# Three reorderings in a two-layer perceiver block: the opening, the last fp4 tile, and a copy in the second attention

## The reference

```
x = x + L0_xattn(ln(x), ctx, ctx, mask)   # 16 heads of 32, 512 keys a batch, projections Wq, Wk, Wv, Wo
x = x + L0_attn(ln(x))                    # RWKV-6 time mix
x = x + L0_ffn(ln(x))                     # gate, up (512 -> 1408), down; fp4 quantise-dequantise of all operands
x = x + L1_xattn(ln(x), ctx, ctx)         # 16 heads of 32, no projections
x = x + L1_attn(ln(x))                    # banded projections, sparse mask
x = x + L1_ffn(ln(x))                     # ternary weights, 512 -> 2048 -> 512
```

## Time and profile before

| | us |
|---|---|
| median of 3 runs | 1557.14 (1554.85 to 1558.16) |
| the profiled execution, its own time | 1559.67 |
| its span, first to last instruction | 1557.9 |
| opening, 0 to 50 | 50 |
| first attention, 50 to 465 | 415 |
| fp4 layer to the start of the second attention, up to | 1142 |
| second attention, from 1142 to | 1317.6 |

### The profile page before, as it was taken

One profiled execution on the slowest core, in us unless ns is written; L12 is line 12 of the kernel. 1 busy time (PEld: TensorE's weight loads), 2 busy tenths in 40 slices (PEclk: granted clock), 3 DMA queues, 4 the chain that ended last, 5 costly groups with the idle time before them and its releaser, 6 DMA issues. The chain is left out here.

```text
span 1557.9 us, 33173 instructions
## 1 busy us (share of the span) xinstructions
PE 1422.0 (91%) x13826; PEld 930.6 (60%) x13826; DVE 1113.0 (71%) x2268; ACT 620.1 (40%) x1285; POOL 183.1 (12%) x179
## 2 busy tenths in 40 slices
PE   6999999999999997999769999999889898978898
PEld 3677777777777776434465644444445555667453
DVE  6477777777787887760497887677558787575787
ACT  2455444554445442223103411110168786034643
POOL 2300000000000000130001000000000001153800
PEclk9999999999999999999989999999899999989999
DMA  6353444444455433400005200000045461040000
GB/s 254 110 178 135 146 148 142 144 146 142 163 171 182 137 107 117 142 1 0 2 27 201 108 1 1 0 0 0 0 163 208 174 229 43 1 165 2 1 28 28
DMA packets 55449, 153.65 MB, mean 99 GB/s; under 512 B 11997, under 2 KB 16861, under 8 KB 49162
## 3 DMA queue, kind: packets, MB, share of 16 engines
q1 hardware_dynamic: 50186, 134.82, 25.0%
q0 software_dynamic: 5120, 16.78, 2.7%
HBM read 117.73 MB, written 33.85 MB: 97 GB/s over the span
## 5 line engine op out<-in xcount | busy, mean ns | idle before, releaser
L744 ACT ACTIVATE l0x_prob<-l0x_prob,l0x_negmax 128x512 f32<-128x512 f32 x128 | 90.9, 712 | 114.8 <-DVE l0x_negmax L818 114.8
L602 PE MATMUL bank<-l0x_upper_v,l0x_ctxT 128*128 128x512 f32 x256 | 106.6, 416 | 2.1 <-DVE l0x_V L797 2.1
L589 PE MATMUL bank<-l0x_ctxT,l0x_upper_k 128*128 128x512 f32 x256 | 106.7, 417 | 1.3 <-PEq L284 1.3
L604 PE MATMUL bank<-l0x_upper_v,l0x_ctxT_lower 128*128 128x512 f32 x256 | 101.6, 397 | 0.0
L603 PE MATMUL bank<-l0x_lower_v,l0x_ctxT 128*128 128x512 f32 x256 | 101.3, 396 | 0.0
L591 PE MATMUL bank<-l0x_ctxT,l0x_lower_k 128*128 128x512 f32 x256 | 100.7, 393 | 0.0
L590 PE MATMUL bank<-l0x_ctxT_lower,l0x_upper_k 128*128 128x512 f32 x256 | 100.2, 391 | 0.0
L1166 DVE CUSTOM_DVE_ANT_0 l1x_prob<-bank,l1x_zeros 128x512 f32<-128x512 f32 x128 | 80.8, 687 | 26.6 <-PE bank L1034 26.0
L1047 PE MATMUL bank<-ident,l1x_prob 128*128 128x128 f32 x512 | 81.5, 289 | 11.9 <-ACT l1x_prob L1117 8.4
L1117 ACT ACTIVATE l1x_prob<-l1x_prob,l1x_negmax 128x512 f32<-128x512 f32 x128 | 91.1, 714 | 1.0 <-DVE l1x_negmax L1166 1.0
L1930 ACT ACTIVATE f_silu<-bank 128x512 f32<-128x512 f32 (+1 forms) x24 | 13.5, 562 | 190.4 <-PE bank L1873 184.1
(11 more groups left out here) (335 smaller groups left out, 3094.1 us busy)
## 6 DMA issues: line engine op xcount, KB each, us to landing
l0x_ctx<-in_ctx SPq DMA_DIRECT2D x16, 1024.0 KB, 5.2
turned_context<-l0x_whole POOLq DMA_DIRECT2D x64, 256.0 KB, 2.4
l1x_KT<-turned_context SPq DMA_DIRECT2D x16, 1024.0 KB, 7.0
l1x_ctx<-in_ctx SPq DMA_DIRECT2D x16, 1024.0 KB, 4.8
fp_weight<-l0x_weight_piece SPq DMA_DIRECT2D x24, 352.0 KB, 4.8
f_raw<-fp_weight SPq DMA_DIRECT2D x3, 2816.0 KB, 18.5
l0x_abs_piece<-in_L_ffn_w_gate SPq DMA_DIRECT2D x16, 512.0 KB, 4.0
l0x_abs_piece<-in_L_ffn_w_up SPq DMA_DIRECT2D x16, 512.0 KB, 5.4
```

Source lines behind the costliest of these rows:

```text
L589: nc.tensor.matmul(bank[:, :], w.upper_k[:, kc, cols], c, start=kc == 0, stop=False)
L602: nc.tensor.matmul(bank[:, :], c, w.upper_v[:, kc, :], start=kc == 0, stop=False)
L604: last = nc.tensor.matmul(bank[:, :], c_lower, w.upper_v[:, kc, :], start=False, stop=kc == CH - 1)
L744: nc.scalar.activation(w.prob[r][:, :], w.prob[r][:, :], ACT.Exp, scale=-1.0, bias=w.negmax[:, p:p + 1], accum_out=w.rowsum[:, b % 2, p:p ...
```

## The change

- The three opening blocks become one, `opening`. Statistics and normalising are done in two halves of four tiles. PE first makes 20 products of a tile of ones, then turns tiles 0 to 3, makes query products 0 and 1, turns tiles 4 to 7, gathers the columns, and goes on with products 2 to 7; the first context turn follows product 2. All eight copies to `g.XNT` are ACT's. The memset of the ones moves here from `projected_attention`.
- The last fp4 tile turns, copies and multiplies its three pieces one after the other (`last_tile`), through the gate banks and into `work[0]`. The rows of tiles 0 to 6 are turned after it. The addition of its sum to `g.X` and the statistics move to the front of DVE's list in `cross_attention`, ahead of the last tile's aggregate.
- In the second attention `heads_copy` stands behind the second exponential on ACT, and `turn_back` behind the second turn on PE.

```diff
@@ -294,30 +287,73 @@
 
         @block.tensor
         def _(pe):
-            def turn(c):
+            def turn_rows(t):
+
+                pe.wait_ge(normed, t + 1)
+                if t >= HALF_TILES:
+                    pe.wait_ge(rows_copied, 2 if t < 6 else t - 1)
+                for c in range(CH):
+                    last = nc.tensor.transpose(g.bank[TURN_BANKS[t]][:, c * P:(c + 1) * P], g.XN[:, t, c * P:(c + 1) * P],
+                                               g.ident[:, :])
+                last.then_inc(rows_turned, 1)
+
+            def turn_context(c):
 
                 pe.wait_ge(w.ctx_loaded[0], 16)
                 if c >= 2:
                     pe.wait_ge(w.whole_ready, c - 1)
+                else:
+                    pe.wait_ge(rows_copied, TILES)
                 for kc in range(KC):
                     last = nc.tensor.transpose(turn_bank[c % 2][:, kc * P:(kc + 1) * P], w.ctx[0][:, kc, c * P:(c + 1) * P],
                                                g.ident[:, :])
                 last.then_inc(turned, 1)
 
-            pe.wait_ge(w.query_weights_loaded, 16)
-            for j in range(8):
+            def query(j):
+
                 oc, half = j % CH, j // CH
+                pe.wait_ge(rows_copied, HALF_TILES * (half + 1))
                 if j >= 6:
                     pe.wait_ge(done, j - 5)
                 for kc in range(CH):
                     last = nc.tensor.matmul(query_bank[j % 6][:, :], w.Wq[:, kc, oc * P:(oc + 1) * P],
                                             g.XNT[:, kc, half * 512:(half + 1) * 512], start=kc == 0, stop=kc == CH - 1)
                 last.then_inc(summed, 1)
+
+
+            pe.wait_ge(w.ones_done, 1)
+            for _ in range(20):
+                nc.tensor.matmul(g.bank[0][:, 0:P], w.ones[:, :], w.ones[:, :], start=True, stop=True)
+            pe.wait_ge(g.ident_loaded, 16)
+            for t in range(HALF_TILES):
+                turn_rows(t)
+            pe.wait_ge(w.query_weights_loaded, 16)
+            query(0)
+            query(1)
+            for t in range(HALF_TILES, TILES):
+                turn_rows(t)
+            pe.wait_ge(g.loaded, 16 * NAMES)
+            for c in range(CH):
+                nc.tensor.transpose(g.bank[3][:, c * 16:c * 16 + NAMES], g.vec[0:NAMES, c * P:(c + 1) * P],
+                                    g.ident[0:NAMES, 0:NAMES]).then_inc(gathered, 1)
+            query(2)
+            turn_context(0)
+            pe.wait_ge(columns_copied, 2)
+            for j in range(3, 8):
...
@@ -331,6 +367,24 @@
 
         @block.vector
         def _(dve):
+            def normalise(half):
+
+                lo, hi = half * HALF_TILES, (half + 1) * HALF_TILES
+                for t in range(lo, hi):
+                    dve.wait_ge(g.x_loaded[t // (TILES // X_PARTS)], 16)
+                    nc.vector.bn_stats(g.stats[:, t, :], g.X[:, t, :]).then_inc(stats_done, 1)
+                dve.wait_ge(stats_done, hi)
+                for t in range(lo, hi):
+                    nc.vector.bn_aggr(g.mean_var[:, t, :], g.stats[:, t, :]).then_inc(aggr_done, 1)
+                dve.wait_ge(aggr_done, hi)
+                nc.vector.tensor_scalar(g.rstd[:, 0, lo:hi], g.mean_var[:, lo:hi, 1], LN_EPS, None, ALU.add).then_inc(var_eps, 1)
+                dve.wait_ge(std_done, half + 1)
+                nc.vector.reciprocal(g.rstd[:, 2, lo:hi], g.rstd[:, 1, lo:hi]).then_inc(rstd_done, 1)
+                dve.wait_ge(rstd_done, half + 1)
+                for t in range(lo, hi):
+                    nc.vector.tensor_scalar(g.XN[:, t, :], g.X[:, t, :], g.mean_var[:, t, 0:1], g.rstd[:, 2, t:t + 1],
+                                            ALU.subtract, ALU.mult).then_inc(normed, 1)
+
             def weight_upper(i, weight):
 
                 dve.wait_ge(w.weight_loaded[i], 16)
@@ -349,6 +403,13 @@
                 dve.wait_ge(w.ctx_upper, c + 1)
                 nc.vector.tensor_tensor(w.ctxT_lower[0][:, c, :], whole[:, :], w.upper[:, :], ALU.subtract).then_inc(w.ctx_lower, 1)
 
+            normalise(0)
+            normalise(1)
+            nc.vector.tensor_copy(g.ident16[:, :], g.ident[:, :]).then_inc(columns_copied, 1)
+            dve.wait_ge(gathered, CH)
+            nc.vector.tensor_copy(g.columns[:, :, 0:NAMES],
+                                  g.bank[3][:, 0:CH * 16].rearrange("p (c n) -> p c n", c=CH)[:, :, 0:NAMES]).then_inc(columns_copied, 1)
+            dve.wait_ge(columns_copied, 2)
             dve.wait_ge(w.mask_rows_loaded, 16)
             nc.vector.tensor_scalar(w.mask_scaled.rearrange("b (c k) -> b c k", c=KC),
...
@@ -1088,9 +1150,9 @@
             scores(0)
             for k in range(QUADS):
                 turn_probabilities(k, 0)
+                turn_probabilities(k, 1)
                 if k % 2 == 1 and k > 1:
                     turn_back(k // 2 - 1)
-                turn_probabilities(k, 1)
                 if k + 1 < QUADS:
                     scores(k + 1)
                 turn_probabilities(k, 2)
@@ -1133,9 +1195,9 @@
             nc.scalar.activation(g.rstd[:, 1, final:TILES], g.rstd[:, 0, final:TILES], ACT.Sqrt).then_inc(last_std, 1)
             for k in range(QUADS):
                 exponential(k, 0)
+                exponential(k, 1)
                 if k % 2 == 1 and k > 1:
                     heads_copy(k // 2 - 1)
-                exponential(k, 1)
                 turned_copy(k, 0)
                 exponential(k, 2)
                 if copied_by_scalar(k, 1):
@@ -1215,6 +1277,10 @@
                     nc.vector.tensor_scalar(g.XN[:, t, :], g.X[:, t, :], g.mean_var[:, t, 0:1], g.rstd[:, 2, t:t + 1],
                                             ALU.subtract, ALU.mult).then_inc(normed, 1)
 
+            nc.vector.tensor_tensor(g.X[:, final, :], g.X[:, final, :], g.bank[6][:, :], ALU.add).then_inc(last_summed, 1)
+            dve.wait_ge(last_summed, 1)
+            nc.vector.bn_stats(g.stats[:, final, :], g.X[:, final, :]).then_inc(last_stats, 1)
+            dve.wait_ge(last_stats, 1)
             nc.vector.bn_aggr(g.mean_var[:, final, :], g.stats[:, final, :]).then_inc(last_aggr, 1)
             dve.wait_ge(last_aggr, 1)
...
@@ -1804,6 +1868,7 @@
         s(f"head_{n}") for n in ("aggr", "eps", "std", "rstd", "normed", "turned", "copied"))
     R = len(N0)
     gate, up, work = g.bank[0:3], g.bank[3:6], g.bank[6:8]
+    LAST_OUT, HEAD_BANKS = work[0], up + gate + [work[1]]
 
     def over_tiles(eng, body):
@@ -1874,23 +1939,41 @@
                                                     start=kc == 0, stop=kc == CH - 1)
                     last.then_inc(gate_up_full, 1)
 
+            def last_tile(t):
+
+                for r, (at, n) in enumerate(N0):
+                    pe.wait_ge(step, t * (R * Q_STEPS) + (r + 1) * Q_STEPS)
+                    for c in range(n // P):
+                        ins = nc.tensor.transpose(gate[r][:, c * P:(c + 1) * P], w.hq[:, at + c * P:at + (c + 1) * P],
+                                                  g.ident[:, :])
+                    ins.then_inc(turn_full, 1)
+                    pe.wait_ge(turned, t * R + r + 1)
+                    for kc in range(at // P, (at + n) // P):
+                        ins = nc.tensor.matmul(LAST_OUT[:, :], w.hT[:, kc * P:(kc + 1) * P], w.downT[:, kc, :],
+                                               start=kc == 0, stop=kc == IC0 - 1)
+                ins.then_inc(out_full, 1)
+                pe.wait_ge(x_done, t)
+                turn_rows()
+
             def turn_rows():
 
                 for t in range(HEAD_TILES):
                     pe.wait_ge(head_normed, t + 1)
                     for c in range(CH):
-                        ins = nc.tensor.transpose(g.bank[t][:, c * P:(c + 1) * P], g.XN[:, t, c * P:(c + 1) * P], g.ident[:, :])
+                        ins = nc.tensor.transpose(HEAD_BANKS[t][:, c * P:(c + 1) * P], g.XN[:, t, c * P:(c + 1) * P], g.ident[:, :])
                     ins.then_inc(rows_turned, 1)
 
             def body(t, first, last, more):
-                if not last:
-                    gate_up(t + 1, False)
+                if last:
+                    last_tile(t)
+                    return
+                gate_up(t + 1, False)
                 pe.wait_ge(step, (t + 1) * (R * Q_STEPS))
                 for r, (at, n) in enumerate(N0):
 
                     if r == 2:
                         pe.wait_ge(turned, t * R + 1)
-                    if r == 0 and not last:
+                    if r == 0:
                         pe.wait_ge(x_ready, t + 2)
                     if r == 1 and not first:
                         pe.wait_ge(x_done, t)
@@ -1902,8 +1985,6 @@
                 if more:
                     turn_tokens(t + 2, work[0])
                 for kc in range(IC0):
-                    if last and kc == TURNS_BEHIND:
-                        turn_rows()
                     ins = nc.tensor.matmul(work[1][:, :], w.hT[:, kc * P:(kc + 1) * P], w.downT[:, kc, :],
```

(35 more changed lines are left out.)

34 lines of the change are left out of this document (10 added, 24 removed).

## The result

The changed kernel takes 1545.77 us, the median of five runs (1542.92 to 1550.22), against 1556.75 of the kernel before in the same session. The ratio is 0.9918, with a 95% interval of 0.9900 to 0.9937: 12.8 us faster by the ratio, 11.0 by the medians. The forecast was 1539.4 and 17.75 less. So the sign and the range hold, the range by a hair (the median lies 0.2 us under its upper end of 1546.0), and about a third of the gain is missing. The profiled execution took 1542.92 (span 1541.1), the fastest of the five.

What follows compares the result with a forecast made beforehand. PE, busy 91%, was taken to wait at the edited places in short chains with another engine or at block edges. Terms -4.9, -7.8, +0.45 and -5.5 sum to -17.75 us: median 1557.14 to 1539.4, range 1534.0 to 1546.0.

Steps and rivals of the forecast that it cites:

- Opening, -4.9: First 50 us: first query product at 11.7 us, not 19.64, last eviction 4.9 us earlier; bounds 2.5 to 5.4.
- Rival (b): Opening pays only 2.5 us, with a lower clock and the DVE, POOL and ACT chain behind: 1541.8 us; chance 0.2.
- Last tile, -7.8: End of the fp4 layer: pieces turned, copied and multiplied one by one; 7.8 us less, bounds 6.0 to 8.5.
- Start of the second attention, +0.45: Front of second attention: the sum delays ACT's first exponential from +2.9 to +3.35; 0.45 us lost, bounds 0 and 1.5.
- Heads, -5.5: Second attention: heads copied after second exponential save 0.4 us a batch, 15 times, 0.5 off: 5.5; bounds 0 and 6.
- Rival (a): Second attention: the reordering pays nothing, since DVE's later heads push back the row maxima; 1544.9 us, chance 0.15.
- rival (c): Second attention: PE's 10.3 us of "issue" stalls grow by half (+5.1, 1544.5 us) or halve (1534.3 us); 0.1 each way.
- The median: Whole kernel: profiled execution, 2.5 us above the median of 1557.14, would take 1541.9, so the median becomes 1539.4.

Runs made afterwards that it cites:

- full_again: The changed kernel run again as it stands: median 1545.69 us, ratio 0.9929 (0.9909 to 0.9948).
- the two shifted ones: The changed kernel with 16 tiny products of ones (64 PE instructions) added behind the 20: 1537.35 us in one run; timed, 1539.62 us, ratio 0.9877.
- no_ones: The changed kernel with one product of ones instead of twenty in the opening: 1540.73 us in one run.
- only_heads: The kernel before with only the heads' copy moved behind the second exponential: median 1555.38 us, ratio 0.9995 (0.9979 to 1.0010).
- the three ratios: The kernel before with one part of the change each: opening 0.9988, last fp4 tile 0.9969, heads' copy 0.9995.
- sum_back: The changed kernel with the last tile's sum and statistics put back at the fp4 layer's end: 1544.22 us, ratio 0.9900 (0.9883 to 0.9917).

## Why the prediction was right, and where it was off

- **Opening, -4.9.** Measured -4.35. The product starts at 11.79 (forecast 11.7), the turns run at 1.97 us for 16, the pace of the upper level, as the ones were to bring about, and the estimate of 2.8 for what lies between the products was some 0.5 short. Rival (b), 2.5, did not come. POOL's first subtraction took 6.09 us instead of 4.51, and the chain still ended ahead of PE.
- **Last tile, -7.8.** Measured -7.82, and the stage takes 274.30 or 274.31 in all ten profiles of kernels with this part. The three sets of 4.8, 4.8 and 3.7 and PE free of waits over 1 us came as worked out, and the root without a drain behind its table load, too (0.01 us).
- **Start of the second attention, +0.45.** This term was mis-sized. The exponential came at +3.4 as predicted, and I priced only that. What I left out is what PE does meanwhile: its scores are short now, it stands 3.12 us, and the stretch at the lower level comes later, over work that waits for PE. The first heads come at +19.50 to +19.78 in the kernels with the old fp4 end and at +20.33 to +21.58 in the whole changed kernel as `full_again`, the two shifted ones, `no_ones` and the first profile show it: +1.2 by the medians (20.82 against 19.62). Three products in the gap kept the level and brought it to +19.00, 1.8 less than that median and 1.3 less than the best of the five, so the cause is shown, in one run.
- **Heads, -5.5.** Measured -5.85 without the stalls. Over 14 intervals with them, -4.67, since stalls took 11.35 us instead of 10.28. Rival (a) is out: DVE keeps 0.19 of slack.
- **The stalls, taken as they were.** This is rival (c), and its reason was right: a shifted program meets them elsewhere. Its counterweight was wrong: I said nothing in the diff adds to PE's stream but 20 products, as if that were little. Those 20 are 80 instructions on PE, ahead of everything, and they moved the blocks of all that follows: the sparse attention, untouched, got two stalls that make 3.7 us and took 1.98 longer (1.95 in `full_again`). The second attention lost 1.1 more between its heads' copies than before, not the 5.1 of the rival. With 64 more the ratio is 0.9877: times the 1557.14 of the start 1538.0, where 1539.4 was forecast. That this comes close to the sum is chance as far as is known: the shifted kernel has stalls of its own, and more of them in the second attention.
- **The median.** This is the largest part of what is missing. I took the profiled execution's 2.5 above its median over to the new kernel. The new one was profiled 2.9 below its own (1542.92 against 1545.77). The profiled pair differs by 16.75, 1.0 less than forecast, and there the 2.4 us that the edited stages lack are made up in part by 1.4 us that the others gained; the medians differ by 11.0. Of the 6.4 us between 1539.4 and 1545.8, more than 5 is this. `only_heads` was profiled 8.7 us below its median, so a forecast of a median from one profile is no finer than several microseconds, and that this one fell inside its range by 0.2 is in part luck.

Open is where the time of the parts went. End to end, the intervals of the three ratios allow 0.5 to 15 us for their sum, and that of the whole 8 to 14, so the noise does not exclude that they add up; it does exclude the 17.9 of the stages. The profiles show each edited stage's gain in each kernel, and changes in unedited stages, by stalls and by the clock, that differ from run to run; which of them the median runs had, one profiled execution each cannot say.

## What to carry to other kernels

Read each edited stage by itself and expect the forecast there to hold to about a microsecond; then expect the whole to lose or win several microseconds by where the code falls in PE's instruction blocks, in stages with bulk transfers and in stages of many short products, and by the level of the clock behind a stand; try a shift of the code before judging a change of under 1%. When a chain ahead of a stage becomes shorter, ask what the engine that used to be slow there now does: the scores finished sooner, PE stood longer, and the clock took back more than the wait cost. A few idle products in such a gap paid for themselves at the first heads' copy.

## What was not expected of the hardware

- What the heads' copies lose to stalls goes from 10.28 to 0.15 us when the transfers beside them are cut, with the same 107 packets in the instruction queue.
- Without bulk transfers PE stalls for instructions too, where it runs through them fast: 1.64, 1.91 and 1.70 us at every 256 of them in wkv.
- PE's level fell behind a stand of 3.12 us (and of 1.81 in `sum_back`), where PE had stood 1.84 at the block's edge and worked 1.12 before it, and stayed low for 6.8 us.
- In the opening of `no_ones` the granted clock column reads 1.00 while the same transposes take twice the time (3.65 us for 16 against 1.97). It reads so for want of a record, which begins at 12.70 us there; the pace alone says that this was the lower level.
- POOL's subtraction of 2048 columns and DVE's next split get in each other's way either way round: before, POOL took 4.51 us and DVE's split 3.46; after, where the split begins 0.5 us behind POOL instead of 2.1, POOL takes 6.09 and the split 1.21. Why they change places is open.
